# Layer 0's first stage of a fused graph and expert network: who writes the normalised rows, VectorE or ScalarE

## The reference, cut to what matters

```python
def _layernorm(x, axis=-1, eps=1e-05):
    m = jnp.mean(x, axis=axis, keepdims=True)
    v = jnp.var(x, axis=axis, keepdims=True)
    return (x - m) / jnp.sqrt(v + eps)

x = x + _L0_gnn_ref(_layernorm(x), adj, ...)   # uses the eigenvectors U of a 64 x 64 Laplacian
x = x + _L0_ffn_ref(_layernorm(x), ...)        # 8 experts, the best 2 of each row
x = x + _L1_gnn_ref(_layernorm(x), adj, ...)
x = x + _L1_ffn_ref(_layernorm(x), ...)
```

## Time and profile before

| | |
|---|---|
| median of 3 runs | 1586.09 us (1583.65 to 1586.94) |
| the profiled execution | 1574.09 us |
| its span (first to last instruction) | 1572.3 us |
| mean granted TensorE clock | 0.892 |
| first stage, by the trace | 324 to 467 us |

### The profile page before, as it was taken

One profiled execution on the slowest core, in us unless ns is written; L12 is line 12 of the kernel. 1 busy time (PEld: TensorE's weight loads), 2 busy tenths in 40 slices (PEclk: granted clock), 3 DMA queues, 4 the chain that ended last, 5 costly groups with the idle time before them and its releaser, 6 DMA issues.

```text
span 1572.3 us, 23783 instructions
## 1 busy us (share of the span) xinstructions
PE 1139.4 (72%) x6494; PEld 945.4 (60%) x6494; DVE 935.4 (59%) x3589; ACT 600.7 (38%) x1663; POOL 628.2 (40%) x610
## 2 busy tenths in 40 slices
PE   4555773268845548999999578987886249999991
PEld 3555762146634436888888333756665238999990
DVE  5776788758873124666677777856542114555673
ACT  3556654025420002222222585655432014444440
POOL 2000000053466664455544500023354675566664
PEclk9999999989957668999999798888898578999996
DMA  9991000000112111222242600000011112222446
GB/s 241 426 427 54 2 0 1 0 1 23 35 43 69 53 57 55 64 63 62 77 115 77 230 1 14 6 23 28 28 48 43 49 58 60 71 74 71 114 120 214
DMA packets 59267, 125.56 MB, mean 80 GB/s; under 512 B 13132, under 2 KB 39636, under 8 KB 57600
## 3 DMA queue, kind: packets, MB, share of 16 engines
q0 software_dynamic: 20000, 73.21, 12.4%
q1 hardware_dynamic: 39136, 50.84, 11.8%
HBM read 50.83 MB, written 74.99 MB: 80 GB/s over the span
## 4 chain that ended last, share of the span: by engine, by line
PE 56%; DVE 14%; issue 10%; another core or an unknown queue 9%; ACT 7%; DMA 2%; POOL 0%; DVEq 0%; SPq 0%; ACTq 0%; POOLq 0%
PE bank L1418 14%; PE bank L1409 8%; PE bank L1406 6%; PE bank L1407 6%; PE bank L1623 4%; PE bank L374 3%; PE bank L192 3%; PE bank L1631 3%; PE bank L1394 2%; PE bank L1578 2%; ACT work L1512 2%; DMA u<-planes 1%; PE bank L805 1%; DVE u L177 1%
## 5 line engine op out<-in xcount | busy, mean ns | idle before, releaser
L1271 POOL DMA_INDIRECT planes<-work,goal x284 | 308.4, 1086 | 278.6 <-DVE work L1330 220.7
L1418 PE MATMUL bank<-pay 128*128 128x128 f32 (+1 forms) x1988 | 292.1, 288 | 94.8 <-issue 59.1
L919 POOL DMA_INDIRECT rows<-pay,slot x256 | 254.0, 992 | 239.5 <-issue 173.4
L1418 PEld LDWEIGHTS bank<-pay 128*128 128x128 f32 (+1 forms) x1988 | 272.8, 200 | 115.0 <-issue 64.1
L1378 ACT ACTIVATE pay<-bank,pay 128x256 f32<-128x256 f32 x284 | 125.5, 475 | 224.4 <-PE bank L1409 95.7
L1374 ACT ACTIVATE pay<-bank 128x256 f32<-128x256 f32 (+1 forms) x213 | 81.1, 383 | 317.7 <-PE bank L1407 175.7
L1409 PE MATMUL bank<-pay 128*128 128x256 f32 x568 | 142.1, 395 | 10.6 <-issue 9.3
L1406 PE MATMUL bank<-pay 128*128 128x256 f32 (+1 forms) x426 | 134.4, 398 | 12.4 <-issue 12.4
L1351 DVE TENSOR_TENSOR pay<-pay,bank 128x256 f32<-128x256 f32 (+1 forms) x213 | 88.6, 418 | 86.8 <-issue 48.7
L1407 PE MATMUL bank<-pay 128*128 128x256 f32 (+1 forms) x426 | 132.6, 394 | 0.0
L192 PE MATMUL bank<-u 63*64 63x2 f32 (+61 forms) x496 | 73.7, 255 | 67.2 <-DVE u L177 66.2
(11 more groups left out here) (401 smaller groups left out, 2047.1 us busy)
## 6 DMA issues: line engine op xcount, KB each, us to landing
rows<-pay POOLq DMA_DIRECT2D x10, 3432.0 KB, 55.9
pay<-rows SPq DMA_DIRECT2D x142, 130.0 KB
u<-planes SPq DMA_DIRECT2D x64, 256.0 KB, 5.0
planes<-work,goal POOLq DMA_INDIRECT x284
wreg<-in_w SPq DMA_DIRECT2D x1, 4264.0 KB, 25.1
wreg<-in_w SPq DMA_DIRECT2D x1, 4112.0 KB, 13.6
X<-in_x SPq DMA_DIRECT2D x2, 2048.0 KB, 20.5
rows<-pay,slot POOLq DMA_INDIRECT x256
```

Source lines behind the costliest of these rows:

```text
L919: return self.nc.gpsimd.indirect_dma_start(out=xs, out_offset=bass.IndirectOffsetOnAxis(ap=self.t["slot"][:, k, q:q + 1], axis=0), in_=sel ...
L1271: nc.gpsimd.indirect_dma_start(out=planes, out_offset=bass.IndirectOffsetOnAxis(ap=t["goal"][:, j * 2 + h:j * 2 + h + 1], axis=0), in_=t[" ...
L1418: ins = T.matmul(ps[4 + j % 2][:, h * P:(h + 1) * P], t["hh"][c][0:n, h * P:(h + 1) * P], t["wst"][j % 2][0:n, at + c * P:at + (c + 1) * P ...
```

## The change

VectorE's four `tensor_scalar` (x minus mean, times reciprocal) are taken out. In their place VectorE makes one small product, off = -mean x reciprocal, for the four groups of a tile, and ScalarE makes the rows as four copies with scale and bias, x times reciprocal plus off. They stand in ScalarE's step between L1148 and L1153. VectorE's reciprocal now also waits until ScalarE has read the reciprocals of the tile before; `sd` grows by one block.

```diff
             A.copy(t["gm"][(s - 1) % 2], ps[2][:, :]).then_inc(S("a0_gm"), 1)
+        if 2 <= s < TILES + 2:
+            act.wait_ge(S("a0_off"), s - 1)
+            for q in range((s - 2) * PAIRS, (s - 1) * PAIRS):
+                ins = A.activation(t["pay"][:, q, 0:P], t["X"][:, q, :], ACT.Identity,
+                                   bias=t["off"][:, q % PAIRS:q % PAIRS + 1], scale=t["sd"][:, 2, q % PAIRS:q % PAIRS + 1])
+            ins.then_inc(S("a0_xh2"), 1)
         if 3 <= s < TILES + 3:
             act.wait_ge(S("a0_t"), s - 2)
...
             dve.wait_ge(S("a0_root"), T + 1)
+            if T >= 1:
+                dve.wait_ge(S("a0_xh2"), T)
             own.chain(V.reciprocal(t["sd"][:, 2, :], t["sd"][:, 1, :]))
-            for q in range(PAIRS):
-                ins = V.tensor_scalar(t["pay"][:, T * PAIRS + q, 0:P], X[:, T * PAIRS + q, :], t["mv"][:, q, 0:1],
-                                      t["sd"][:, 2, q:q + 1], ALU.subtract, ALU.mult)
-            ins.then_inc(S("a0_xh2"), 1)
+            V.scalar_tensor_tensor(out=t["off"], in0=t["mv"][:, :, 0], scalar=-1.0, in1=t["sd"][:, 2, :],
+                                   op0=ALU.mult, op1=ALU.mult).then_inc(S("a0_off"), 1)
...
             if T >= 1:
-                dve.wait_ge(S("a0_xh2"), T)
+                dve.wait_ge(S("a0_off"), T)
             V.tensor_tensor(xt, xt, pairs(ps[3][:, :]), ALU.add).then_inc(S("a0_xadd"), 1)
...
-        t["bn"], t["mv"], t["sd"] = sb("bn", [P, PAIRS, 6]), sb("mv", [P, PAIRS, 2]), sb("sd", [P, 3, PAIRS])
+        t["bn"], t["mv"], t["sd"] = sb("bn", [P, PAIRS, 6]), sb("mv", [P, PAIRS, 2]), sb("sd", [P, 4, PAIRS])
+        t["off"] = t["sd"][:, 3, :]
```

## The result

The change made the kernel slower: 1596.84 us median (1589.9 to 1606.27, 8 runs) against 1584.05 us for the kernel before (1582.66 to 1592.54, 8 runs), ratio 1.0081 with a 95% interval of 1.0051 to 1.0111. The forecast was 1578.1 us, between 1572 and 1584. The profiled execution of the kernel before that the prediction used was itself a short one (1574.09 us); the eight executions timed beside the changed kernel lie 8.6 to 18.5 us higher.

A forecast was written before the change was run, and what follows sets the result against it. VectorE was taken to bound the long steps, with TensorE's output bounding the short ones. Long steps 6.0, step 2 2.0 and short steps 0 made 8.0 us, so 1586.1 - 8.0 = 1578.1 us, range 1572 to 1584.

The forecast's parts named there:

- ScalarE's delay for free: Copies add 1.55 us a tile on ScalarE; taken as 0, at most 1.5 us lost in all.
- the third: Rival: long step's output matmul L1126 is caught in the hold, 3.0 us a step, all six 1596 us; chance 0.10.
- The long steps' 6.0 us: Seven long steps (odd steps 5 to 15, and 17): VectorE freed of 0.86 us each, 6.0 us in all.
- The short steps: Sum bound by copy, matmul and unnamed wait (0.69 us in step 12); gain taken as 0, upper bound 2.6 us.
- Step 2: First stage, sum starts earlier once the 4.47 us normalisation leaves VectorE; 2.0 us gained, bounds 1.4 and 2.3.
- the 1.02 that I allowed for: Small `tensor_scalar` L1031, 1.02 us in step 1; if slowed likewise in step 2, 0.85 us is lost.
- rival 1: TensorE's clock stays at 2.4 GHz once its idle gap (343.98 to 358.38) closes: 4 us more, 1574 us; chance 0.14.
- rival 2: Short steps' waits grow by the 0.86 us each long step gives; 2.9 us stay, 1583.2 us; chance 0.15.

The follow-up runs named there:

- experiment 4: Kernel before, plus four scaled copies a tile of other data into a spare place on ScalarE; ratio 1.0036, 1575.90 against 1572.62 us.
- experiment 17: The changed kernel unaltered, timed a fourth time against the kernel before; ratio 1.0061, first stage 152.9 us.
- experiment 5: The kernel before once more, unaltered, for the spread of its profiles; first stage 145.1 us.
- 14: The kernel before, unaltered, profiled on one more chip, with late results; first stage 144.0 us.
- Experiment 6: The changed kernel once more, unaltered, for the spread of its profiles; first stage 151.5 us.
- 13: The changed kernel unaltered, against the kernel before on one more chip, with late results; ratio 1.0059, first stage 154.9 us.
- Kernel 9: Changed kernel with only the tiles of steps 2 to 5 on ScalarE, others on VectorE; against the kernel before 0.9977 without late results, 0.9952 with them.
- experiment 15: Changed kernel, real scatters put after the stage, beside it the same rows as indirect DMAs in order to a spare tensor; first stage 162.1 us.
- experiment 1: Changed kernel with ScalarE's four copies moved behind the relu (L1164); against the kernel before ratio 1.0035, 1574.25 against 1572.62 us.
- 10: Kernel before with each group's scatters started behind the short step's sum; ratio 0.9999 on the chip without late results, first stage 134.2 us.
- kernel 11: Changed kernel, copies behind the relu, scatters behind the short step's sum; against the kernel before 0.9877 without late results, 1.0059 with them.

## Why the prediction was wrong

**The step that failed** is the one that took ScalarE's delay for free: "The next step is long, where the output has 3.7 us of slack." The slack was read from the earlier trace rows, but it holds only as long as TensorE's results reach ScalarE at once. In the kernel before, L1107 of step 11 ended at 402.83, 1.9 us after the first scatter of its group, and L1148 started at once:

```profile
401.77 1.06 PE L1107 MATMUL bank<-small,u 128*128 128x128 f32 x8
403.04 0.59 ACT L1148 COPY u<-bank 128x512 f32<-128x512 f32 x1
400.88 0.97 POOL L919 DMA_INDIRECT rows<-pay,slot  x1 [5.14 <-issue]
```

In the changed kernel it ended at 406.24, 4.6 us after the first scatter (401.64), and L1148 waited 4.45 us. I put the shift of 2.7 us down to ScalarE's 1.55 and VectorE's 0.9 in the gates, both on paths that I had costed at nothing; no run takes it apart. What the runs show in place of the free delay: from step 6's root on the changed kernel takes 27 to 31 us more with scatters beside it than without, the kernel before 2 to 10, and the delay alone (experiment 4) has a ratio of 1.0036.

**The rival that came true** was the third, with a chance of 0.10 and 1596 us; 1596.84 was measured. Its place was off by one step: not the output L1126 was caught but L1107 ahead of it, so that the output matmul itself started late (for step 7 it was L1121 of step 6, ahead of L1164). Its price of 3.0 us a step was about right (3.04 in step 7, 4.38, 3.06, 3.31 and 3.46 in the next four long ones). That the number fits to 1 us is luck all the same: it counted six long steps, but step 5 has no scatter beside it; it counted nothing for the short steps, which lost 6.6 us; and it started from 1586.1 us, where the eight runs have a median of 1584.05. I weighed it low because of "a shift of 2.4 at worst, most of which the roots absorb"; the shift of L1107 against the scatters was 2.7 us, so they absorbed none of it.

**The long steps' 6.0 us** were about right where nothing is late: 8.66 to 7.72 us a step, 0.94 in place of 0.86. **The short steps**, taken as nothing, give 0.76 us each there (5.76 to 5.00). The 0.69 us ahead of the sum of step 12, the reason for the nothing, is 0.24 in the kernel before once the scatters are gone: it was mostly the late result.

**Step 2** did not give its 2.0 us. In the changed kernel's first profile its sum starts only 0.3 us earlier than before (341.37 against 341.69). VectorE there:

```profile
338.17 0.73 DVE L1181 SCALAR_TENSOR_TENSOR sd<-mv,sd 128x4 f32<-128x4 f32 x1
341.37 0.69 DVE L1195 TENSOR_TENSOR X<-X,bank 128x512 f32<-128x512 f32 x1 [2.47 <-PE bank L1126]
...
343.41 2.84 DVE L1031 TENSOR_SCALAR sd<-mv 128x4 f32<-128x4 f32 x1
```

The product took 0.73 instead of 0.16 us, while GpSimd's additions ran (333.94 to 346.23). That agrees with the rule of the Trainium skill ("SBUF — State Buffer", section "Who interferes with whom") that two SBUF inputs are blocked by a reading GpSimd. L1031 took 2.84 us and ended together with the additions, more than the 1.02 that I allowed for. In experiment 17 the sum of step 2 did start 2.3 us earlier, at 339.38, and L1031 took it all back. VectorE and GpSimd there:

```profile
341.42 4.95 DVE L1031 TENSOR_SCALAR sd<-mv 128x4 f32<-128x4 f32 x1
```

```profile
326.74 19.61 POOL L1225 TENSOR_TENSOR X<-X,work 128x512 f32<-128x512 f32 x16
```

L1031 ends at 346.37, the last addition at 346.35. In step 2 of the kernel before L1031 takes 0.2 us in every profile, since L1174 stands ahead of it and has met the additions in its place (4.47 us). So the collision moved from one instruction to the next. On average step 6's root starts at 365.1 us in the six profiles in which VectorE normalises all tiles and at 364.8 in the twelve in which ScalarE does: 0.3 us where 2.0 was forecast.

**The clock** (rival 1) held up between steps 3 and 4 in the first profile: from 343.98 to 358.38 it was 1.00, where it had been 0.65, and these steps took 5.00 and 5.61 us from root to root, against 6.79 and 7.61. In its other profiles the kernel before had 0.88 (experiment 5) and 0.64 (14) in that stretch, and the changed one 1.00, 1.00 and 0.76 (6, 13 and 17), so it is not the same in every execution.

The Trainium skill's page "Perfetto Trace Analysis", section "Optimizing Scalar/DVE Operations", says that moving work to ScalarE may make sense if VectorE is saturated. Taken strictly, as in rival 2, this left 3.3 us of gain. Without late results the short steps gained too, 0.76 us each, so taken that way it was too cautious here, and the loss had another cause.

## What to carry to other kernels

An engine freed of work moves everything that hangs on it: ask which transfers start sooner and what then falls into their time. Slack that is read from a trace holds only for the present order of the transfers; a wait whose releaser the trace can't name is a resource of its own and must be priced before anything is moved into its reach. Where a transfer is the trouble, one can try to take the gain only in the steps that have none beside them. Kernel 9 does so and was 0.2 and 0.5% faster, though its profiles don't show that the gain lies there. And a close sum is no proof of its terms: here 8.5 us came in for 8.0 forecast, with the short steps and step 2 off by 4.6 and 4.8 us in opposite directions.

## What the hardware showed that was not expected

- While indirect DMAs run, results of TensorE can reach the waiting engine late; the longest such wait of ScalarE in these stages is 5.88 us (experiment 15). Plain DMAs of the same rows, by either queue, bring none (one profile each). When the lateness begins varies: 3.7 us after the group's first scatter a result was still in time (L1098 of step 11 in the changed kernel, over at 405.35, read at 405.86), while in experiment 1 one that was over 2.6 us after it (L1115 at 404.76, scatter at 402.16) was read only at 406.43.
- The late results are not all held until the group is through. In the twelve profiles that have them, 96 waits of ScalarE in the first stage are ended by "remote", 79 of them within 0.2 us of 4.3, 5.7, 7.2, 8.6, 10.0 or 11.5 us after their group's first scatter. That is a step of about 1.43 us, and the last is eight such steps, with eight scatters in a group. So results seem to get through about once per scatter, and a step can pay several times. Experiment 6 has two in one step; GpSimd's first scatter and ScalarE, 5.74 and 11.50 us behind it:

```profile
418.92 0.97 POOL L919 DMA_INDIRECT rows<-pay,slot  x1 [7.77 <-issue]
```

```profile
424.66 0.59 ACT L1148 COPY u<-bank 128x512 f32<-128x512 f32 x1 [2.38 <-remote]
430.42 0.69 ACT L1164 ACTIVATE u<-bank,small 128x512 f32<-128x512 f32 x1 [2.24 <-remote]
```

  By what mechanism is not settled.
- Not every chip shows it. On one no result was late in any of four profiles, and the same kernel took 1395.8 us instead of 1571 to 1588, 12% less. Nearly all of it is saved where indirect DMAs run: between the profiles of 14 and 10, two versions of the kernel before, layer 0's experts take 73 us less (397.2 against 324.0), while the mixing part of layer 1, with no indirect DMA beside it, takes 65.4 and 64.4. Whether the chip or its state at the time makes the difference wasn't tried; the same chip number gave medians of 1572.62 and 1587.52 us for the kernel before at two times. A change tuned under one condition can turn round under the other: kernel 11 is 1.2% faster there and 0.6% slower here.
